# A macaron block of two feed-forward layers around a Mamba layer: a new order of a round's steps, five SiLU products on GpSimd, the convolution's history as a bias of ScalarE

## The reference

```python
x = x + 0.5 * ffn(layernorm(x));  x = x + mamba(layernorm(x));  x = x + 0.5 * ffn(layernorm(x))

# ffn: mixes each token with the one before it
xr = mu_r * x + (1 - mu_r) * x_prev;  xk = mu_k * x + (1 - mu_k) * x_prev
out = sigmoid(xr @ W_r.T) * (relu(xk @ W_k.T) ** 2 @ W_v.T)

# mamba: normalizes again, adds its own input at the end
xs, z = split((layernorm(x) * ln_w + ln_b) @ W_in.T)        # 1024 channels each
xc = silu(b_conv + sum(xs[t - 3 + k] * W_conv[:, k] for k in range(4)))
dt_low, B, C = split(xc @ W_x.T)                            # 32, 16, 16
delta = softplus(dt_low @ W_dt.T + b_dt)
h[t] = exp(delta * A) * h[t-1] + delta * B[t] * xc[t]       # 16 states for each of 1024 channels
y[t] = sum_n(h[t, n] * C[t, n]) + D_skip * xc[t]
out = (y * silu(z)) @ W_out.T + residual
```

## Time and profile before

| | |
|---|---|
| median of 3 runs | 5162.35 us |
| profiled execution, its own time | 5150.87 us |
| span of its trace | 5148.8 us |
| DVE busy | 4517.2 us, 88% |
| PE busy | 4319.5 us, 84% |
| POOL busy | 3145.4 us, 61% |
| ACT busy | 2903.8 us, 56% |
| granted TensorE clock, mean share of full | 0.932 |

### The profile page before, as it was taken

The page is one execution under the profiler, slowest core; times in us unless marked ns, Lnnn a source line. Parts: engine busy times, 40 slices in busy tenths (PEclk is TensorE's granted clock), DMA queues, the critical chain, the costliest instruction groups (busy, mean ns, idle before and its releaser), DMA issues.

```text
span 5148.8 us, 57715 instructions
## 1 busy us (share of the span) xinstructions
PE 4319.5 (84%) x16640; PEld 2441.2 (47%) x16640; DVE 4517.2 (88%) x3778; ACT 2903.8 (56%) x6355; POOL 3145.4 (61%) x3200
## 2 busy tenths in 40 slices
PE   5676989888898988889798888978889898888777
PEld 2344545455454544545454454545445454454443
DVE  1589999998998999899999998999999899989982
ACT  2455655666565656655565555566656555665551
POOL 1366757566675766657576665657667575666660
PEclk8788999999999999999999999999999999999788
DMA  1356556465654656555565655646566564654551
GB/s 61 103 144 175 166 149 179 139 186 156 168 188 132 187 149 184 165 159 167 158 181 158 180 166 149 177 140 194 151 179 180 133 184 148 182 165 140 164 153 59
DMA packets 423052, 810.69 MB, mean 157 GB/s; under 512 B 41264, under 2 KB 41264, under 8 KB 418640
## 3 DMA queue, kind: packets, MB, share of 16 engines
q1 hardware_dynamic: 422736, 807.00, 54.3%
HBM read 772.25 MB, written 34.60 MB: 157 GB/s over the span
## 4 chain that ended last, share of the span: by engine, by line
PE 49%; DVE 28%; issue 11%; ACT 7%; DMA 3%; POOL 2%; SPq 0%; DVEq 0%; POOLq 0%; ACTq 0%
DVE decay L1030 11%; PE y_acc L491 10%; PE mm L407 9%; PE mm L418 8%; DVE g L1038 7%; PE mm L514 6%; PE mm L443 4%; DVE xc L990 4%; PE mm L433 3%; PE mm L396 3%; DMA c_all<-bc_scratch 3%; PE mm L455 2%; DVE mix_k L963 1%; POOL dbx L1244 1%; ACT L771 1%
## 5 line engine op out<-in xcount | busy, mean ns | idle before, releaser
L1244 POOL TENSOR_TENSOR dbx<-u,b_all 128x1024 f32<-128x1024 f32 x1024 | 2412.8, 2356 | 1534.4 <-DVE g L1038 1528.6
L1030 DVE TENSOR_TENSOR_SCAN decay<-decay,state,dbx 128x1024 f32<-128x1024 f32 x1024 | 2405.9, 2350 | 299.7 <-ACT decay L823 288.9
L491 PE MATMUL y_acc<-ident,g 128*128 128x128 f32 x8192 | 1175.7, 290 | 550.2 <-DVE g L1038 490.3
L491 PEld LDWEIGHTS y_acc<-ident,g 128*128 128x128 f32 x8192 | 997.6, 149 | 1076.4 <-DVE g L1038 747.1
L1038 DVE TENSOR_TENSOR g<-decay,c_all 128x1024 f32<-128x1024 f32 x1024 | 1245.0, 1216 | 13.2 <-DMA c_all<-bc_scratch 0.9
L820 ACT ACTIVATE decay<-delta,neg_a 128x512 f32<-128x512 f32 x1024 | 708.7, 692 | 36.8
L823 ACT ACTIVATE decay<-delta,neg_a 128x511 f32<-128x511 f32 x1024 | 687.0, 671 | 0.0
L829 ACT ACTIVATE state<-decay 128x2 f32<-128x2 f32 x1024 | 168.4, 164 | 644.9 <-DVE g L1038 644.7
L418 PE MATMUL mm<-wbuf_c,col 128*128 128x512 f32 x1024 | 460.7, 593 | 12.0 <-ACT delta L771 12.0
L735 ACT ACTIVATE xc<-mm,evec,conv_sb 128x512 f32<-128x512 f32 x128 | 99.5, 777 | 358.5 <-PE mm L433 343.8
L990 DVE SCALAR_TENSOR_TENSOR xc<-mm,conv_sb,xc 128x509 f32<-128x509 f32 (+2 forms) x384 | 287.4, 749 | 13.6
(11 more groups left out here) (98 smaller groups left out, 5111.7 us busy)
## 6 DMA issues: line engine op xcount, KB each, us to landing
b_all<-bc_scratch SPq DMA_DIRECT2D x1024, 256.0 KB, 3.9
c_all<-bc_scratch SPq DMA_DIRECT2D x1024, 256.0 KB, 4.5
wbuf_c<-in_w_v SPq DMA_DIRECT2D x32, 1024.0 KB, 8.1
wbuf_d<-in_w_r SPq DMA_DIRECT2D x16, 1024.0 KB, 8.0
xin<-in_x SPq DMA_DIRECT2D x16, 1024.0 KB, 6.5
wbuf_c<-in_w_k SPq DMA_DIRECT2D x16, 1024.0 KB, 7.9
wbuf_d<-in_w_in SPq DMA_DIRECT2D x16, 1024.0 KB, 7.9
wbuf_a<-in_w_in SPq DMA_DIRECT2D x16, 1024.0 KB, 10.3
```

The lines of the kernel that those rows point to most:

```text
L491: last = pe.matmul(y_acc[:, tb, j * P:(j + 1) * P], g[:, s % PAIRS, j, tb * P:(tb + 1) * P], ident[:, :], start=n == 0 and j == 0 and tb % ...
L1030: dve.tensor_tensor_scan(d, d, flat(dbx[:, s % DBX, :, :]), state[:, batch, s, 0:1], ALU.mult, ALU.add).then_inc(scan_done, 1)
L1244: pool.tensor_tensor(dbx[:, s % DBX, :, :], u[:, q % 2, :, :], b_all[:, s % BRING, :].unsqueeze(1).broadcast_to([P, QT, W]), ALU.mult).the ...
```

## The change

It leaves what is computed as it is and touches four things.

1. **Five of eight SiLU products go to POOL.** For tiles 2 to 6 ACT adds 1 to the tanh itself (`one{e}`, a second pass over 512 columns), and POOL multiplies in slots 39, 41, 43, 45 and 47. DVE keeps tiles 0, 1 and 7, now in slots 33, 34 and 46.
2. **The history comes in as a bias of ACT.** The instruction of line 982 is gone. ACT's first pass covers columns 3 to 511, and three passes of one column each take `head` as their bias; POOL adds b_conv to `head` with one more instruction.
3. **The order in the slots.** Among others: xs goes from slots 30, 32, 35, ... 45 to 28, 30, 34, ... 44; z0 to z3 from 25, 26, 31, 36 to 27, 29, 35, 37; dt_proj for quarter 2 with its softplus from 14 and 15 to 18 and 19, for quarter 3 from 34 and 35 to 33 and 34, for quarter 0 of the next chunk from 50 and 51 to 55 and 56; ffn_turn of the second layer from 33 to 32; z4 from 58 to 53; the norms' statistics on DVE one by one. The load of `wbuf_a` for xs stays in slot 26. `GROUPS` gets the new order and other bank numbers.
4. **The banks take turns where there is no scan.** In round -1 xs uses the banks in turn (`TURNS`), and so do ffn_turn, ffn_k and ffn_r in round 16.

```diff
+        TURNS = {-1: {f"xs{e}": e % 2 for e in range(ET)},
+                 NCH: {f"f1{q}{n}": n % 2 for q in "Tkr" for n in range(CT)}}
+
+        def home(it, group):
+            return TURNS.get(it, {}).get(group, GROUPS[NUMBER[group]][4])
...
             def conv_start(k, e, batch):
-                act.activation(xc2[:, e, :], bank(f"xs{e}"), ACT.Identity, scale=conv_sb[:, e, KC - 1:KC],
+                src = bank(k - 1, f"xs{e}")
+                act.activation(xc2[:, e, HIST:W], src[:, HIST:W], ACT.Identity, scale=conv_sb[:, e, KC - 1:KC],
                                bias=evec[:, 0, e:e + 1]).then_inc(m_act.sem, 1)
-                act.activation(xs_last[:, batch, e, :], bank(f"xs{e}")[:, W - HIST:W],
-                               ACT.Copy).then_inc(m_act.sem, 1)
+                for c in range(HIST):
+                    act.activation(xc2[:, e, c:c + 1], src[:, c:c + 1], ACT.Identity,
+                                   scale=conv_sb[:, e, KC - 1:KC],
+                                   bias=head[:, e, c:c + 1]).then_inc(m_act.sem, 1)
+                act.activation(xs_last[:, batch, e, :], src[:, W - HIST:W], ACT.Copy).then_inc(m_act.sem, 1)
...
             def conv_tanh(k, e):
+                t = rows[0][:, e % TB, :]
+                act.activation(t, xc2[:, e, :], ACT.Tanh, scale=0.5).then_inc(m_act.sem, 1)
+                if 2 <= e < 7:
+                    act.wait_ge(m_act.sem, m_act.at(k, f"th{e}"))
+                    act.activation(t, t, ACT.Identity, bias=1.0).then_inc(m_act.sem, 1)
...
             def conv_taps(k, e):
                 dve.wait_ge(m_act.sem, m_act.at(k, f"last{e}"))
-                dve.wait_ge(m_pool.sem, m_pool.at(k, "h4"))
-                dve.tensor_tensor(xc2[:, e, 0:HIST], xc2[:, e, 0:HIST], head[:, e, :],
-                                  ALU.add).then_inc(m_dve.sem, 1)
...
+            def conv_silu(k, e):
+
+                pool.wait_ge(m_act.sem, m_act.at(k, f"one{e}"))
+                o = xc2[:, e, :]
+                pool.tensor_tensor(o, rows[0][:, e % TB, :], o, ALU.mult).then_inc(s_pool.sem, 1)
...
             def xproj(it, k, part):
-                pe.wait_ge(m_dve.sem, m_dve.at(k, f"silu{4 * part + 3}"))
+                pe.wait_ge(s_pool.sem, s_pool.at(k, f"{3 + 3 * part}"))
...
-                    if front and s in (30, 32, 35, 37, 39, 41, 43, 45):
-                        xs(it, f, (30, 32, 35, 37, 39, 41, 43, 45).index(s), other)
+                    if front and s in (28, 30, 34, 36, 38, 40, 42, 44):
+                        xs(it, f, (28, 30, 34, 36, 38, 40, 42, 44).index(s), other)
```

More of the change, by code:

```diff
@@ L203, in bank_free, with bank @@
+        def home(it, group):
+            return TURNS.get(it, {}).get(group, GROUPS[NUMBER[group]][4])
+        def bank(it, group):
+            return mm[:, home(it, group), :]
         def bank_free(it, group):
-            n, home = NUMBER[group], GROUPS[NUMBER[group]][4]
-            while True:
+            n, mine = NUMBER[group], home(it, group)
+            while it >= -2:
                 n -= 1
@@ L379, in turn_rows @@
                     pe.wait_ge(*free)
-                o = bank(group)
+                o = bank(it, group)
                 for tb in range(TB):
@@ L432, in xs @@
                 for ct in range(CT):
[L433 removed]
+                    last = pe.matmul(bank(it, f"xs{e}"), win[:, ct, e % 4 * P:(e % 4 + 1) * P], xn_col[:, slot, ct, :],
                                      start=ct == 0, stop=ct == CT - 1)
@@ L442, in z @@
                 for ct in range(CT):
-                    last = pe.matmul(bank(f"z{e}"), win[:, ct, e % 4 * P:(e % 4 + 1) * P], xn_col[:, slot, ct, :],
+                    last = pe.matmul(bank(it, f"z{e}"), win[:, ct, e % 4 * P:(e % 4 + 1) * P], xn_col[:, slot, ct, :],
                                      start=ct == 0, stop=ct == CT - 1)
@@ L513, in out_proj @@
                 for e in range(4):
-                    last = pe.matmul(bank(f"o{tb}"), gate[:, 4 * part + e, tb * P:(tb + 1) * P], wo[:, e, :],
+                    last = pe.matmul(bank(it, f"o{tb}"), gate[:, 4 * part + e, tb * P:(tb + 1) * P], wo[:, e, :],
                                      start=part == 0 and e == 0, stop=part == 1 and e == 3)
@@ L695, in ffn_tanh @@
                 act.wait_ge(f_pe[i].sem, f_pe[i].at(k, f"r{tb}"))
-                act.activation(rows[i][:, tb, :], bank(f"f{i}r{tb}"), ACT.Tanh,
+                act.activation(rows[i][:, tb, :], bank(k - (1, -1)[i], f"f{i}r{tb}"), ACT.Tanh,
                                scale=0.5).then_inc(f_act[i].sem, 1)
@@ L808, in gate_tanh @@
                     act.wait_ge(y_pe.sem, count)
-                act.activation(gate[:, e, :], bank(f"z{e}"), ACT.Tanh, scale=0.5).then_inc(z_act.sem, 1)
+                act.activation(gate[:, e, :], bank(k, f"z{e}"), ACT.Tanh, scale=0.5).then_inc(z_act.sem, 1)
             def make_decay(it, s):
@@ L923, in body @@
                         keep_y(it, 2)
-                    if back and s == 50:
-                        ffn_tanh(1, b, 0)
-                    if front and s == 51:
+                    if back and 50 <= s < 54:
+                        ffn_tanh(1, b, s - 50)
+                    if scn and s == 54:
+                        gate_tanh(it, 4)
+                    if front and s == 56:
                         softplus(f, 0, 0)
@@ new lines, in body @@
+                    if back and s in (36, 37):
+                        ffn_mix_k(1, b, 2 * (s - 36))
+                        ffn_mix_k(1, b, 2 * (s - 36) + 1)
+                    if back and s in (38, 40):
+                        ffn_mix_r(1, b, s - 38, xin)
+                        ffn_mix_r(1, b, s - 37, xin)
+                    if scn and s == 54:
+                        gate_silu(it, 4)
+                    if back and s in (55, 57, 58, 59):
+                        ffn_gate(1, b, (55, 57, 58, 59).index(s))
@@ L1100, in body @@
+                    if ahead and 56 <= s < 60:
+                        if s == 56:
                             if due(count := f_pool[0].at(it + 1, "mean")):
```

337 lines of the change are left out of this document (163 added, 174 removed).

## The result

The changed kernel takes 5144.05 us (median of 12 runs, 5139.04 to 5153.96) against 5154.26 us of the kernel before (12 runs in turn with them, 5151.07 to 5166.75): a ratio of 0.9981, interval 0.9972 to 0.9990. That is 10 us faster, just at the bound of what can be told from no change, where the prediction had 5064 us and a range from 5005 to 5130. The direction of the forecast holds by a hair, its size does not: nine tenths of the gain are missing. The 12 runs also put the kernel before 8 us lower than the three that the prediction started from (5162.35).

What follows compares the result with a forecast made beforehand. DVE bounds the kernel, with PE close behind. Middle rounds -60, round 0 -4, round 15 0, first round -29, last -4.5: -98 us on 5150.9, 5053, carried over to 5064 us; 8 in 10 for 5005 to 5130.

Steps and rivals of the forecast that it cites:

- First round: Round -1: with two banks xs tiles come 5.0 to 6.6 us apart; with transposes and x projection, -29 us in all.
- Slots 0 to 29: Middle round: -1.1 us by slot 26 from moved softplus, and some 3 us of waits gone at slot 28 and turn_y.
- The stall: Slot 29: PE stands 6 us at xs0 for wbuf_a's load, DVE idles about 6 us, plus 1.3 us of slow PE.
- the walk: Reckoning of a middle round by start times, stretch by stretch: -4.3 us a round, between -8 and 0.
- the pair of waits in slots 34 and 35: ffn_turn on one bank and the softplus behind it: 2.41 + 3.17 us before, 1.5 + 1.5 foreseen, one slot earlier.
- Slots 35 to 47: Middle round: DVE sheds 3 products and 6 histories, ACT's passes fit beside it; from +0.8 to -5.8 us.
- I cost it at nothing: Slots 39 to 47: POOL's SiLU products, 1.27 us each, cost nothing, as POOL waits 96 us a round.
- Rival D: POOL and DVE hinder each other: each POOL product holds DVE up 1.27 us, +102 us, 5166 us; chance 0.04.
- Slots 47 to 63: Middle round: PE binds before and after, so the lead of 5.8 us is kept, -5.6 at the round's end.
- Rival C: Slot 29: a stall long enough to make the kernel slower; 16 us of it make +30, 5193 us; chance 0.06.
- B: Rival: saved work becomes longer waits for decay, only first and last round gain, -34 us, 5128 us; chance 0.15.
- over 303 us a middle round: Sign that the forecast of a 301 us middle round is wrong, as is one under 298 us.

Runs made afterwards that it cites:

- e1_turns: The kernel before, in its own order, with only the bank turns for round -1's xs and the last chunk's ffn1 groups: 5103.0 us, ratio 0.9896.
- e4_nopool: The changed kernel with all eight SiLU products on DVE again and without ACT's five passes that add 1: 5133.5 us, ratio 0.9956.
- e6_history: The changed kernel with the history added on DVE again and ACT's three one-column passes gone: 5178.9 us, ratio 1.0051.
- e9_order: The changed kernel with SiLU products and history both back on DVE, leaving the new order and bank turns: 5166.8 us, ratio 1.0008.
- e2_load: The changed kernel with xs0's load of wbuf_a issued in slot 25, ahead of wbuf_b's load, instead of slot 26: 5084.8 us, ratio 0.9860.
- e7_norm: e2_load with ACT's norm of ffn1's rows in slot 31 put behind the start of xs1's convolution: 5038.3 us, ratio 0.9778.
- e3_mixes: The changed kernel with ffn1's mixes on DVE moved to slots 37, 39 and 41, away from POOL's products: 5180.1 us, ratio 1.0046.
- e10_mixes_ring: e7_norm with six of eight xs put ahead of sum_g on PE, and the mixes moved as in e3_mixes: 4980.4 us, ratio 0.9651.

## Why the prediction was wrong, step by step

Of the 98 us of gain that the profiled execution was to show, 97 are missing in the fourteen middle rounds (+37 instead of -60); round 0 (+4 instead of -4) is made good by the first round and the end. So the account goes by the stretches of a middle round.

- **First round: right, a little small.** Expected -29, measured -34.8. The tiles came 4.5 to 5.1 us apart, at and below the lower end of the 5.0 to 6.6 given, since PE, which waited less, ran at its high clock (3.67 us a group). Round 15 and what follows gave -7 where -4.5 was expected. e1_turns shows what was not seen: the banks alone bring -44 in the first round, and the rest of the change takes 9 of them back (POOL's products 2.7, by e4_nopool, the columns 2.9, by e6_history, and the order 3.2, from e1_turns to e9_order).
- **Slots 0 to 29: right in sum, less so in its parts.** -4.2 against -4.1. Slots 14 to 26 gave -0.4 instead of -1.1, slots 26 to 29 -3.5 instead of -3.
- **Slots 29 to 35: the step that failed first, by a size.** The stall was foreseen with its cause, place and PE's standing time (6 us, measured 5.4), and it cost about what was booked for it, 6 us for DVE plus 1.3 of clock. DVE's wait was 8.5, since PE's standing is followed by the whole of xs0 at the low clock, 2.2 us longer, and by ACT's passes; but removing it and the wait that it hid (e2_load, e7_norm) shortens the stretch by 7.6 us. What failed is the rest of the stretch. In e7_norm, without the stall, slots 0 to 35 gain 2.2 us, where the walk without its 7.3 would have them gain 5.2. Two of these 3 us are the pair of waits in slots 34 and 35, which the walk let shrink to 3.0 us because a SiLU product stands in each slot; it stayed at 4.9 (5.1 in e7_norm). By e2_load the stall ends when the load is issued a slot earlier. The wait behind the store in slot 31, 3.1 us, was not in the walk at all; it showed only when the first stall was removed.
- **Slots 35 to 47: the step that failed worst, and the one that was argued.** The walk has -6.6 us, measured -3.5. "I cost it at nothing" was said of POOL's product, for POOL. For POOL it was right: it waits as long for g as in the earlier trace rows, by the waits of that round in the changed kernel.
```profile
POOL dbx L1268 <- DVE g L1053: 94.5, 47, 7.5
```
The price lay with DVE: 3 x 1.07 us in the mixes. Rival D had looked for it in the scan and in g, found them free of it, rightly, and got 0.04; I had not listed what else of DVE reads two SBUF tiles in slots 36 to 40. The row was there: the product of two SBUF tiles at 1.00 us, with POOL's dbx beside it, where the same product with nothing of POOL beside it takes 0.68 and the mean of the earlier trace rows mixes both. The Trainium skill (SBUF — State Buffer, SBUF: two separate sides) says that whichever of the two engines starts first holds the shared ports for its whole instruction and the other is blocked. The runs agree: a pair of mixes beside a product of 1.27 us took 1.07 us longer, and g beside one, whose decay is not in SBUF, none; who started first can't be read from the trace, where the two start within 0.01 us. The walk had a second thing wrong in this stretch: it called these slots DVE's own. e3_mixes took the 1.07 us off all three pairs and the kernel became slower, because PE's ring through xs, with PE slower in it, then set the pace. Only with the ring opened do the mixes give their 3.2 us back (e10_mixes_ring), and then the stretch stands at -7.2 us against the kernel before, where the walk had -6.6.
- **Slots 47 to 63:** +1.1 instead of +0.2. The wait at slot 57 came as foreseen (1.6 us), but not in place of those at slots 50 to 54, which are 6.7 us a round instead of 5.7.
- **Rival C** had the right place (slot 29) and B nearly the right gain in the first and last round (-34, measured -42), each with a wrong mechanism for the rest. What happened was a part of C (a stall of 8.5 us) and a part of D (1.07 us, for three products of five). By "over 303 us a middle round" the forecast had named its own failure correctly.

What stays open is slots 31 to 35. They are 1.9 us longer in the fastest kernel (34.8 us from slot 29 to 35) than in the one before (32.9), its scans of slots 34 and 35 still wait 2.7 us each for decay, and PE runs there at a granted clock of 0.76 on average, where 0.5 and 1 are its two levels of 1.2 and 2.4 GHz (a window of it, slots 30 to 35, columns as above):
```profile
2062.71:2098.68 35.97, 26.97 (x109) 17.25 (x108) 28.18 (x24) 25.36 (x57) 18.43 (x16) 0.76 0.51 141
```
No run took the second ffn's transposes, ACT's copies of them and the softplus behind apart, so how much of these waits is the clock's and how much the single bank's is not known.

## What to carry to other kernels

When an order written out by hand moves a consumer ahead, move the load that it waits for by as many slots, and read which instruction is queued behind each wait on the way; a stall of one engine hides the next one. Work given to an idle engine is priced by what runs beside it on the engine it was taken from: list the instructions there that read two SBUF tiles, and put it beside others. And an edit's worth is the worth in its surroundings: moving the mixes lost 36 us in one order of the other engines and gained 47 in another, so undo and do a part in both before it is judged.
